# Block products for the last two weight tiles, four rows of h kept in DRAM, and Prelu chains for the last down units

## The reference

```
Wg, Wu (1792 x 512), Wd (512 x 1792) = 16-level codes -> table value, times one factor per 64 entries
K   = S4 kernel of length 512 from Lambda, p, q, Vc, Ct, B, step
out = x + (causal convolution of xn with K, along the 512) + D*xn
        + (silu(xn Wg^T) * (xn Wu^T)) Wd^T
```

## Time and profile before

| | |
|---|---|
| time of 3 runs | 469.8 us median (469.63 to 470.71) |
| profiled execution, span | 469.1 us, 7151 instructions |
| granted clock, mean | 1.000 |
| VectorE busy | 84% |
| ScalarE busy | 61% |
| SyncE's DMA traffic | 38.81 MB, mean 83 GB/s |
| chain that ended last, TensorE's share | 68% |

### The profile page before, as it was taken

The page is one execution under the profiler, slowest core; times in us unless marked ns, Lnnn a source line. Parts: engine busy times, 40 slices in busy tenths (PEclk is TensorE's granted clock), DMA queues, the critical chain, the costliest instruction groups (busy, mean ns, idle before and its releaser), DMA issues.

```text
span 469.1 us, 7151 instructions
## 1 busy us (share of the span) xinstructions
PE 450.1 (96%) x2607; PEld 255.0 (54%) x2607; DVE 395.9 (84%) x651; ACT 284.8 (61%) x475; POOL 31.1 (7%) x88
## 2 busy tenths in 40 slices
PE   0699999999999999999999999999999999999997
PEld 0554444444444444444444444466544688888886
DVE  4899669978798687988999558878899999999993
ACT  7986686487597765769778555884222543545340
POOL 0400385000000000000001000000000000000000
PEclk9999999999999999999999999999999999999999
DMA  8382545112223112212132215346500021001111
GB/s 277 83 287 70 113 82 151 47 57 80 67 68 91 46 45 68 67 46 92 45 112 69 92 22 143 100 135 203 184 1 0 1 91 46 30 16 47 46 46 45
DMA packets 30166, 38.81 MB, mean 83 GB/s; under 512 B 12916, under 2 KB 14004, under 8 KB 30132
## 3 DMA queue, kind: packets, MB, share of 16 engines
q1 hardware_dynamic: 30132, 38.37, 27.3%
HBM read 31.74 MB, written 4.52 MB: 77 GB/s over the span
## 4 chain that ended last, share of the span: by engine, by line
PE 68%; DVE 8%; issue 1%; DMA 1%; ACT 1%; DVEq 0%; ACTq 0%
PE bank L1819 27%; PE bank L2053 20%; PE bank L1948 16%; PE bank L1996 4%; DVE work L1695 2%; DVE h L1707 1%; DMA xT<-in_x 1%; DVE work L1700 0%; DVE work L1703 0%; DVE work L1714 0%; DVE work L1089 0%; DVE work L1698 0%; DVE wd L1707 0%; DVE work L1697 0%; PE bank L1907 0%
## 5 line engine op out<-in xcount | busy, mean ns | idle before, releaser
L1819 PE MATMUL bank<-xT,w 128*128 128x512 f16 (+1 forms) x828 | 184.9, 379 | 2.2 <-DVE w L1099 1.7
L1819 PEld LDWEIGHTS bank<-xT,w 128*128 128x128 f16 x828 | 81.5, 99 | 98.5 <-DVE w L1099 2.1
L735 ACT ACTIVATE work<-work 128x512 f32<-128x512 int32 x152 | 86.5, 621 | 3.4 <-DVE work L1075 1.9
L2053 PE MATMUL bank<-wd,work 128*128 128x256 f16 x504 | 56.3, 273 | 0.4 <-DVE work L1714 0.4
L2053 PEld LDWEIGHTS bank<-wd,work 128*128 128x128 f16 (+1 forms) x504 | 49.2, 98 | 6.6 <-DVE work L1714 0.7
L1035 ACT ACTIVATE work<-h 128x896 f16<-128x896 f32 x30 | 28.0, 943 | 29.2 <-DVE h L1727 21.6
L2053 PE MATMUL bank<-h,work 128*128 128x256 f16 x378 | 42.2, 273 | 0.0
L801 ACT ACTIVATE work<-bank,sc 128x512 f32<-128x512 f32 x47 | 31.7, 677 | 16.7 <-PE bank L1819 15.3
L2053 PEld LDWEIGHTS bank<-h,work 128*128 128x128 f16 x378 | 37.0, 98 | 4.3
L1948 PE MATMUL bank<-h 128*128 128x512 f16 x150 | 36.4, 379 | 0.2 <-issue 0.2
L2006 PE MATMUL bank<-wd,h 128*128 128x512 f16 x168 | 36.6, 379 | 0.0
(11 more groups left out here) (193 smaller groups left out, 562.9 us busy)
## 6 DMA issues: line engine op xcount, KB each, us to landing
h<-in_x SPq DMA_DIRECT2D x8, 512.0 KB, 5.7
xT<-in_x SPq DMA_DIRECT2D x16, 256.0 KB, 4.4
out<-xT SPq DMA_DIRECT2D x15, 256.0 KB, 2.1
work<-in_q_gate SPq DMA_DIRECT2D x14, 256.0 KB, 2.8
work<-in_q_up SPq DMA_DIRECT2D x14, 256.0 KB, 2.7
work<-in_am_gate SPq DMA_DIRECT2D x28, 128.0 KB, 2.9
work<-in_am_up SPq DMA_DIRECT2D x28, 128.0 KB, 3.1
work<-in_q_down SPq DMA_DIRECT2D x14, 256.0 KB, 2.8
```

Source lines behind the costliest of these rows:

```text
L735: nc.scalar.activation(knee_of(u, k), qs[:, u % 2, :], KNEE, scale=scale, bias=bias, alpha=below).then_inc(knee_done, 1)
L1819: mm = nc.tensor.matmul(out_b, weights(k)[:, unit, wl, f, :], xT[:, TPC * c + first:TPC * c + last, xl, f, :], start=(i == 0), stop=(i == ...
L2053: mm = nc.tensor.matmul(out_b, part, w, start=(n == 0), stop=(n == 3 * KT - 1))
```

## The change

What the diff does:

- `BLOCKED` becomes 3 to 13: tiles 12 and 13 go through the blocked window too. Tile 11 uses the common rooms for its sums.
- Rows 0 to 3 of h (tiles 0 to 3) are written to DRAM (`h_out`, one at the first unit of each of the windows of tiles 5 to 8, 1 MB each). The results of tiles 10 to 13 go to rows 0 to 3 (`HOME`). The four moved rows come back into rows 10 to 13 in four parts by chunk (`h_back`, 1 MB each), behind the last block product. The down tiles are taken in the order that this gives (`TILE`).
- `EARLY_IN` gets a sixth entry: tile 6's window makes three units. Tile 13's makes three and not four. Four units stay for behind it. `DOWN_ROWS` sets the order of the down rows.
- The last four down units are `CHAINED`: two chains of Prelu passes, four and three long, seven in all on ScalarE, in place of four passes and a clamp; VectorE does WHOLE and SCALED only. ScalarE's part is made in the items of the unit before, as the Prelu passes were.
- Waits at the start of the convolution follow the banks that the blocked window leaves last.
- The order of the stages, and of slots and joins in a blocked window, is as it was.

```diff
-BLOCKED = range(3, 12)
+BLOCKED = range(3, NM)
-EARLY_IN = (5, 9, 10, 11, 12)
+EARLY_IN = (5, 6, 9, 10, 11, 12)
-LAST_UNITS = 4
+LAST_UNITS = 3
+DOWN_ROWS = (0, 1, 2, 3, 4, 12, 5, 6, 7, 8, 9, 10, 11, 13)
+CHAINED = range(UNITS - 4, UNITS)
+MOVED = 4
+HOME = [mt if mt < NM - MOVED else mt - (NM - MOVED) for mt in range(NM)]
...
+            def h_out(mt):
+                sp.wait_ge(h_done, max(len(OPENING), NCH * (mt + 1)))
+                sp.wait_ge(hlo_done, SPLIT * max(3, mt + 1))
+                sp.dma_start(moved[:, mt, :], h_f32[:, mt, :]).then_inc(moved_st, 16)
+            def h_back(c):
+                if c == 0:
+                    sp.wait_ge(m_done, len(BLOCKS) * len(BLOCKED))
+                    sp.wait_ge(moved_st, 16 * MOVED)
+                part = slice(CH * c, CH * (c + 1))
+                sp.dma_start(h_f32[:, NM - MOVED:NM, part], moved[:, :, part]).then_inc(moved_ld[c], 16)
...
+                for mt in range(MOVED):
+                    if place == made_before(5 + mt):
+                        h_out(mt)
+            h_back(0)
             absmax_of(UNITS - 3)
-            load_residual(0, 2)
+            load_residual(0, 1)
             codes_of(UNITS - 2)
-            load_residual(2, 3)
             absmax_of(UNITS - 2)
-            load_residual(3, 4)
+            load_residual(1, 3)
             codes_of(UNITS - 1)
-            load_residual(4, 8)
+            load_residual(3, 7)
             absmax_of(UNITS - 1)
-            load_residual(8, NT)
+            load_residual(7, 9)
+            h_back(1)
+            load_residual(9, NT)
+            h_back(2)
+            h_back(3)
...
+            def chain_pass(u, j):
+                side, i = CHAIN_ORDER[j][0], int(CHAIN_ORDER[j][1])
+                room = chain_room(u, side)
+                if i == 0:
+                    act.wait_ge(q_ld[u % 2], 16 * (u // 2 + 1))
+                    if u - 1 in CHAINED:
+                        act.wait_ge(dq_done, dq_after(u - 2, WHOLE))
+                    else:
+                        act.wait_ge(dq_done, dq_after(u - 1, LEFT))
+                else:
+                    act.wait_ge(knee_done, PASSES_AT[u] + CHAIN_ORDER.index(f"{side}{i - 1}") + 1)
+                scale, bias, below = (RIGHT_CHAIN if side == "r" else LEFT_CHAIN)[i]
+                nc.scalar.activation(room, room if i else qs[:, u % 2, :], KNEE, scale=scale, bias=bias,
+                                     alpha=below).then_inc(knee_done, 1)
...
             for k in range(3, NM):
-                if k in BLOCKED:
-                    blocked_window(k)
-                for c in range(0 if k in BLOCKED else NCH):
-                    n = NCH * k + c
-                    bank_free(n)
-                    if c == 3 and k == NM - 2:
-                        pe.wait_ge(t_done, 1)
-                    products(n)
+                blocked_window(k)
...
             for mt in range(NM):
-                pe.wait_ge(wlo_done, PLACE[GU + mt] + 1)
+                pe.wait_ge(wlo_done, PLACE[GU + DOWN_ROWS.index(mt)] + 1)
+                if mt == NM - MOVED:
+                    pe.wait_ge(moved_ld[0], 16)
```

More of the change, by code:

```diff
@@ L115, in made_in, with eighths @@
     return 2 + (k in EARLY_IN) if k < NM - 1 else LAST_UNITS
+def eighths(at, k, e):
+    n, rest = divmod(made_in(k) * e, 8)
+    u = made_before(k) + n
+    return at[u] + (at[u + 1] - at[u]) * rest // 8 if rest else at[u]
 FIRST = SPLIT * TPC
 KT = NM // 2
+MOVED = 4
+HOME = [mt if mt < NM - MOVED else mt - (NM - MOVED) for mt in range(NM)]
+TILE = [r + (NM - MOVED) if r < MOVED else r if r < NM - MOVED else r - (NM - MOVED) for r in range(NM)]
 FH = HD // 2
@@ L442, in ffn_conv_kernel @@
         room_free = sem("room_free")
+        moved_st = sem("moved_st")
+        moved_ld = [sem(f"moved_ld{c}") for c in range(NCH)]
         wb_done = sem("wb_done")
@@ L831, in block_hi @@
                 w_sums = sums_room(k)[1]
-                first, last = sums_parts(k)[part]
+                first, last = SUMS_PARTS[part]
                 nc.scalar.activation(sums_split(k, first, last)[:, :, HI].rearrange("p i f m -> p i (f m)"),
@@ L969, in _, with window @@
             block_hi(BLOCKED[0], 1)
[L970 to L972 removed]
+            items(ACT_AT[8] + 1, ACT_AT[9] - 3)
+            def window(k):
                 n = NCH * k
+                if k == NM - MOVED:
+                    act.wait_ge(moved_st, 16 * MOVED)
                 def part(first, last):
[L976 removed]
+                    items(eighths(ACT_AT, k, first), eighths(ACT_AT, k, last))
                 silu(n)
@@ L1101, in items @@
             def items(first, last):
-                for p in range(first, min(last, DVE_ITEMS * UNITS)):
-                    u, i = p // DVE_ITEMS, p % DVE_ITEMS
+                for p in range(first, last):
+                    u, i = item_of(DVE_AT, p)
+                    if u in CHAINED:
+                        i += 2
                     if i != 2:
@@ L1499, in window @@
-                for c in range(NCH):
-                    n = NCH * k + c
+                n = NCH * k
+                if k == NM - MOVED:
+                    dve.wait_ge(moved_st, 16 * MOVED)
+                if k == BLOCKED[0]:
                     h_mul(n)
-                    items(at + per * 2 * c // 8, at + per * (2 * c + 1) // 8)
-                    if stage:
-                        stage(2 * c)
                     h_lo(n)
-                    items(at + per * (2 * c + 1) // 8, at + per * (2 * c + 2) // 8)
-                    if stage:
-                        stage(2 * c + 1)
+                    stage_of(0, 2)
+                    join(k, 0)
+                    stage_of(2, 4)
+                else:
+                    stage_of(0, 2)
+                    h_mul(n)
+                    stage_of(2, 3)
+                    h_lo(n)
+                    stage_of(3, 4)
+                    join(k, 0)
@@ L1510, in _ @@
+                stage_of(4, 6)
+                join(k, 1)
+                h_mul(n + 3)
+                stage_of(6, 7)
+                h_mul(n + 1)
+                stage_of(7, 8)
+                block_of(other_sums, k + 1)
+                block_of(block_lo, k + 1, 0)
+                h_mul(n + 2)
+                block_of(block_lo, k + 1, 1)
             for k in range(3, NM - 7):
```

187 lines of the change are left out of this document (83 added, 104 removed).

## The result

| | median, us | executions | ratio to the kernel before | 95% interval |
|---|---|---|---|---|
| before | 470.63 (469.45 to 474.71) | 18 | 1 | |
| changed | 473.52 (470.51 to 476.15) | 18 | 1.0062 | 1.0046 to 1.0078 |

The change costs 2.9 us. Forecast were 470.7 us and a cost of 0.85, with a range to 472.4; the result is outside it. The kernel before ran with a median of 469.8 in the three runs shown then and of 470.63 in all 18, so 0.8 of the distance is the base. By the ratio alone the changed kernel would have come to 472.7 on the old base, still outside.

What follows compares the result with a forecast made beforehand. TensorE was taken to bound the kernel, with VectorE's path 0.4 us later where they meet at the end. The terms -2.58 + 3.46 + 0.38 - 0.41 = +0.85 on 469.8 gave 470.7 us, range 466.6 to 472.4.

Steps and rivals of the forecast that it cites:

- TensorE saves 2.58 us in two windows: Windows of tiles 12 and 13: blocked ones have 90 matmuls, plain ones 96, saving 2.58 us if nothing waits.
- The Toeplitz stall, 3.46 us: Tile 12's window: VectorE waits for `T` before the join, so TensorE's product 4 starts 3.46 us late.
- Second stall 0.38 us: Tile 13's window: product 5 waits 0.38 us for VectorE's `block_lo`, bounds 0 and 1.2.
- Wait of 0.41 goes: Second block product at the end: TensorE's 0.41 us wait for VectorE's low part disappears.
- Does VectorE hold the end?: After the convolution: VectorE's weight sums start at 342.0, may start as late as 343.1, so TensorE does not wait.
- Nothing for these: Rows coming back on SyncE's queue (`h_back`) arrive before their readers need them: no cost.
- Rival 3: End goes over to VectorE: `h_back(1)` delays the last residual by 4 us, giving 473.6 us; chance 0.06.
- Rival 2: Behind tile 12's product 4 the stall lowers TensorE's clock, costing 1.4 us more, giving 472.1 us; chance 0.12.
- The base: Whole kernel before the change: the runs' median of 469.8 us, 0.7 above the profiled span, to which +0.85 was added.

Runs made afterwards that it cites:

- both: Changed kernel with the line written to DRAM once, then copied into 128 rows, and the second 1 MB of rows queued behind the residuals: 467.85 us, ratio 0.9941.
- hback_last: Changed kernel with the second 1 MB of rows coming back queued behind the last residual load, not in front of residuals 9 to 15: 471.58 us, ratio 1.0023.
- stage_late: Changed kernel with VectorE's Toeplitz steps moved behind the join, to slots 6, 7 and the next window's slot 0, same DMA: 472.50 us, ratio 1.0039.
- late_hback: Changed kernel with VectorE's Toeplitz steps behind the join and the second 1 MB of rows behind the residuals, line's copy unchanged: 468.06 us, ratio 0.9946.

## Why the prediction was wrong, step by step

- *TensorE saves 2.58 us in two windows.* Right; it is what `both` has.
- *The Toeplitz stall, 3.46 us.* Right in place, engine, order and cause. The sizes seen are 2.15 and 3.54, as the copy took 11.7 and 13.3 us. I had taken one duration of a DMA for fixed.
- *Second stall 0.38 us.* Measured 0.47.
- *Wait of 0.41 goes.* Right in the number, by luck. The weight sums start at 343.59, past both the 342.0 forecast and the 343.1 that the prediction could bear: 36.3 us behind the start of the convolution, against 32.1 in `both`. There is no wait only because TensorE was late by 2.17 us itself; without that it would have waited some 1.5 us here (an estimate: 343.59 + 29.97 = 373.56 for the low part, against 371.90 - 2.17 + 2.3 = 372.0).
- *"Does VectorE hold the end?"*, and "Nothing for these" of the rows coming back. **This is the step that failed.** I asked when the last residual lands and when the weight sums start, and for `h_back(1)` only when its own reader needs it. But it stands in front of residual 9, whose addition frees the bank of the second down product: TensorE comes there 26 us behind the start of the convolution and lost 2.17 us waiting for such banks, a term that the sum had at nothing. Rival 3 had the right queue and the wrong reader, and a chance of 0.06; the delay of the last residual that it feared, 4 us, was there too, covered as said above. `hback_last` took 1.9 us away by moving one line, and its 471.6 would have been inside the range.
- *Rival 2, the clock, 0.12.* It was true together with the forecast, in seven to 11 of 18 executions (seven at the 0.996 of `hback_last` and `stage_late`, four at the 0.993 that the kernel before shows too). Its price was read from matmuls at full clock. It was set up as an alternative; it should have been a term of the sum, as its cause is the very stall of 3.46 us that I forecast. That the trace before showed 1.00 everywhere said only that it had no such wait behind its start.
- *The base.* Three runs gave 469.8, more gave 470.6, and the executions' times lie 1.5 to 1.9 us over their spans in every result, not 0.7. The base moved the number by 0.8 and the measured difference not at all.

So the sum ought to have been -2.58 + 2.15 to 3.54 + 0.47 + 2.17 - 0.58, and up to 1.7 for the clock: +1.6 to +4.7, where 2.9 was measured. The main gain exists and the change can be had with it: `both` and `late_hback` beat the kernel before by 0.5 to 0.6%.

How much a single execution's stall varies with the copy, and what makes it take 11.7 or 13.3 us, stays open. That the low clock follows a TensorE wait is shown by three profiled executions (waits of 3.4, 3.45 and 16.5 us) and the counts; that the executions without a profile are low for the same reason is argued from the counts only. The one profiled execution with 0.993 has its low stretch at the kernel's start, so part of the counts may be that.

## What to carry to other kernels

A step moved in front of another on an in-order engine must be checked against every wait that it contains: here a reader of a DMA came to stand before a join, and the DMA had been on time only for the old order. For a transfer put on a queue, ask not when its reader needs it but who stands behind it. When a forecast has TensorE idle for several microseconds, add the price of a lower clock behind it to the sum, not to the rivals.

## What was not expected of the hardware

- 256 KB from four SBUF partitions, 128 times over, take 11.7 to 13.3 us; the same bytes from one row in DRAM, with the 128 copies outermost, 4.0 us. Two DMAs, one behind the other (6.4 us together), were quicker than one.
- A wait of TensorE of 3.5 us is followed by a granted clock of 0.55 and 0.81 over the next 5.7 us, a cost of 1.7 us; one of 16.5 us, within which the clock had fallen already, by 0.50 for 5 us and 0.79 for the next 3, a cost of 2.85; one of 2.15 us left it at 1.00.
- The 1 MB read into SBUF beside the residuals landed some 8 us after its issue (median of the page), against 5.0 for the 1 MB written.
